# Two-layer cross-attention: the first layer's score products in two key halves of 128 instead of one of 256

## The reference, cut to what matters

```python
h = jnp.concatenate([x, latents], axis=1)
q = (latents @ q_w + q_b).reshape(b, k_len, NH, DH)
kv = (h @ kv_w + kv_b).reshape(b, p + k_len, NH, DH, 2)
kmat, v = (kv[..., 0], kv[..., 1])
attn = jnp.einsum('bkhd,bnhd->bhkn', q, kmat) / DH
full_mask = jnp.concatenate([attention_mask.astype(bool), jnp.ones((b, k_len), bool)], axis=-1)
attn = jnp.where(full_mask[:, None, None, :], attn, -jnp.inf)
attn = jax.nn.softmax(attn.astype(jnp.float32), axis=-1).astype(q.dtype)
attn_out = jnp.einsum('bhkn,bnhd->bkhd', attn, v).reshape(b, k_len, H)
```

## Time and profile before

| what | us |
|---|---|
| median of three runs | 1155.17 |
| profiled execution, its own time | 1155.72 |
| its span, first to last instruction | 1153.5 |
| TensorE busy with products in the span | 1078.4 |
| VectorE, ScalarE, GpSimd busy | 690.8, 648.5, 321.7 |
| first attention | 0 to about 480 |

### The profile page before, as it was taken

One profiled execution on the slowest core, in us unless ns is written; L12 is line 12 of the kernel. 1 busy time (PEld: TensorE's weight loads), 2 busy tenths in 40 slices (PEclk: granted clock), 3 DMA queues, 4 the chain that ended last, 5 costly groups with the idle time before them and its releaser, 6 DMA issues. The chain is left out here.

```text
span 1153.5 us, 27390 instructions
## 1 busy us (share of the span) xinstructions
PE 1078.4 (93%) x8976; PEld 912.7 (79%) x8976; DVE 690.8 (60%) x2683; ACT 648.5 (56%) x2204; POOL 321.7 (28%) x507
## 2 busy tenths in 40 slices
PE   5899999999999998599999999999978999999994
PEld 4788888888888886489899989998966877777772
DVE  4577777777777777562122112211337999999994
ACT  4545555555555555373333333333428999999993
POOL 1223333333333333200000000000001455555555
PEclk9999999999999999789999999999999999999997
DMA  8211111212111110275011010110211212221200
GB/s 287 76 40 49 50 49 57 63 53 65 48 48 48 48 46 10 82 236 158 1 55 54 2 55 19 35 55 1 74 37 59 70 52 67 77 77 50 66 22 28
DMA packets 65355, 71.16 MB, mean 62 GB/s; under 512 B 7056, under 2 KB 41104, under 8 KB 65296
## 3 DMA queue, kind: packets, MB, share of 16 engines
q1 hardware_dynamic: 65296, 70.42, 19.2%
HBM read 49.43 MB, written 20.97 MB: 61 GB/s over the span
## 5 line engine op out<-in xcount | busy, mean ns | idle before, releaser
L727 POOL TENSOR_TENSOR pr<-pr,rec 128x512 f32<-128x512 f32 x128 | 130.6, 1042 | 295.8 <-DVE rec L993 295.8
L1496 ACT ACTIVATE pr<-pr,nmax 128x128 f32<-128x128 f32 x512 | 198.2, 396 | 1.5 <-DVE nmax L1584 1.5
L1926 ACT ACTIVATE g_m<-J,b_part_m 128x256 f32<-128x256 f32 x128 | 60.7, 474 | 216.6 <-PE J L175 216.6
L832 ACT ACTIVATE pr<-pr,nmax 128x256 f32<-128x256 f32 x256 | 126.6, 501 | 3.5 <-DVE nmax L982 3.4
L1584 DVE CUSTOM_DVE_ANT_0 pr<-S,madd 128x128 f32<-128x128 f32 x512 | 114.0, 282 | 2.2 <-issue 1.2
L1903 POOL TENSOR_TENSOR resid_m<-resid_m,b_all_m 128x512 f32<-128x512 f32 x16 | 22.3, 1410 | 326.6 <-DMA resid_m<-in_x 326.6
L1496 ACT ACTIVATION_READ_ACCUMULATOR pr<-pr,nmax 128x1 f32 x512 | 100.2, 196 | 0.0
L982 DVE CUSTOM_DVE_ANT_0 pr<-S,madd 128x256 f32<-128x256 f32 x256 | 92.5, 418 | 8.3 <-PE S L1176 8.1
L175 PE MATMUL J<-nT0hi_m,uphi 128*128 128x256 f32 x256 | 73.0, 285 | 8.5 <-DVE uplo L163 5.1
L175 PE MATMUL J<-hThi,wkhi 128*128 128x256 f32 x256 | 74.8, 292 | 0.8 <-DVE wklo L157 0.8
L175 PE MATMUL J<-nT0hi_m,uplo 128*128 128x256 f32 x256 | 72.6, 284 | 0.0
(11 more groups left out here) (236 smaller groups left out, 3233.6 us busy)
## 6 DMA issues: line engine op xcount, KB each, us to landing
staged<-in_L_xattn_mlp_w SPq DMA_DIRECT2D x16, 512.0 KB, 4.4
rows<-in_ctx SPq DMA_DIRECT2D x16, 256.0 KB, 2.8
rows<-in_x SPq DMA_DIRECT2D x16, 256.0 KB, 3.0
kept_c<-hThi SPq DMA_DIRECT2D x16, 256.0 KB, 2.7
kept_c<-hTlo SPq DMA_DIRECT2D x16, 256.0 KB, 2.8
kept_n<-n_out SPq DMA_DIRECT2D x16, 256.0 KB, 2.4
n_in<-kept_n SPq DMA_DIRECT2D x16, 256.0 KB, 3.8
resid_m<-in_x SPq DMA_DIRECT2D x16, 256.0 KB, 2.9
```

Of the source, the lines that this page charges most:

```text
L727: pool.tensor_tensor(part, part, by.unsqueeze(2).broadcast_to([P, per_bank, keys]), ALU.mult).then_inc(normed, 1)
L832: last = nc.scalar.activation(part, part, ACT.Exp, bias=nmax[slot][:, at], scale=-1.0, accum_out=den[slot][:, at])
L1496: last = nc.scalar.activation(pr[k][:, i, :], pr[k][:, i, :], ACT.Exp, bias=nmax[k][:, i:i + 1], scale=-1.0, accum_out=den[r][:, at:at + 1])
L1926: nc.scalar.activation(g[slot][:, :], J[j][:, 0:PR], ACT.Gelu_apprx_tanh, bias=b1_part[:, f, :]).then_inc(J_taken[j], 1)
```

## The change

In the first layer, `scores` writes each product of 256 keys as two of 128 keys. The two halves are the outer loop: for each c, first all three passes and four strips for keys 0 to 127 (columns 0 to 127 of the head's part of the bank), then the same for keys 128 to 255. The stationary operand is the same in both. The last pass of c = 1 and of the second half raises `S_full[j]`. The products of a round go from 24 to 48, each with its own load of the stationary operand. The branch for L = 1 in this function is not used, since the second attention has its own code.

```diff
@@ -1169,15 +1169,17 @@
                     for c in range(RC):
-                        for qh, kh in PASSES:
-                            for j in range(SB):
-                                strip = slice(32 * j, 32 * (j + 1))
-                                k_ap = KT[s][kh][strip, RC * r + c, :] if L == 0 else KT[s][kh][strip, :, :]
-                                mm = nc.tensor.matmul(S[j][:, c * 256:(c + 1) * 256],
-                                                      QT[s][qh][strip, RC * r + c, :], k_ap,
-                                                      start=(qh, kh) == PASSES[0], stop=(qh, kh) == PASSES[-1])
-                                if c == RC - 1 and (qh, kh) == PASSES[-1]:
-                                    mm.then_inc(S_full[j], 1)
+                        for part in range(2):
+                            for qh, kh in PASSES:
+                                for j in range(SB):
+                                    strip = slice(32 * j, 32 * (j + 1))
+                                    at = slice(part * P, (part + 1) * P)
+                                    k_ap = KT[s][kh][strip, RC * r + c, at] if L == 0 else KT[s][kh][strip, part, :]
+                                    mm = nc.tensor.matmul(S[j][:, c * 256 + part * P:c * 256 + (part + 1) * P],
+                                                          QT[s][qh][strip, RC * r + c, :], k_ap,
+                                                          start=(qh, kh) == PASSES[0], stop=(qh, kh) == PASSES[-1])
+                                    if (c, part) == (RC - 1, 1) and (qh, kh) == PASSES[-1]:
+                                        mm.then_inc(S_full[j], 1)
```

## The result

The changed kernel takes 1172.99 us, the median of four runs (1171.99 to 1176.02), against 1154.63 us for the kernel before in the same comparison (1152.41 to 1156.08). The ratio is 1.0155, with a 95% interval from 1.0132 to 1.0179, so the medians differ by 18.4 us and the interval runs from 15 to 21 us. The forecast was 1172.3 us.

The account below looks back on a forecast made before the run. TensorE was taken to bound the kernel; 32 score rounds at +0.55 us give +17.6 us, less 0.5 hidden, +17.1 on the 1155.17 us median: 1172.3 us, range 1164 to 1184.

Parts of the forecast that it names:

- TensorE bounds the first attention: Steady stretch, 60 to 425 us: TensorE busy 357.99 of 365 us, so a microsecond of its work is one of time.
- A set costs the longer of stream and load: Score rounds: each set costs its stream (0.12 us for 256 columns) or the next set's load (0.11), whichever is longer.
- The 0.11 read from the first two sets of loads: Start of a score round: loads 0.11 us apart with nothing streaming, taken as the price of each 128-key set.
- The lower bound of 0.06: Cost of a 128-key score set from below: 0.06 us, its stream, if loads shrink or hide as the transposes' allow.
- The lead-in: Start of a score round: 0.10 us for the first set's loads until its stream begins.
- the lead-out: End of a score round, last set to next operation: 0.23 us less 0.06 for half a stream, 0.17.
- All 32 rounds count: First attention, prologue and end included: every score round pays +0.55 us, +17.6 us in all.
- Little is hidden: Wait for VectorE's V behind round 0: absorbs some 1.1 us at most over 14 entries; 0.5 us taken.
- The fallback to plain float32: Rival, score sets: narrow fp32r runs at plain float32 rate, 0.22 us a set, +56 us, 1211 us; chance 0.12.
- The hidden loads: Rival, score sets: loads don't bind, a set costs its 0.06 us stream, 1155 to 1156 us; binding less or not 0.07.
- the rule by which load and stream add up: Trainium skill on score sets: loads overlap products only in different row groups; estimated +0.66 us a round or +21 us.
- The 81 ns for a pair of load and product: Skill's middle case for score sets: 0.081 us each, round 1.16 us, +7 us, 1162 to 1163 us.

Follow-up runs that it names:

- the run with quarters: Against the kernel before, each score product of 256 keys written as four of 64 keys in both rounds; 1259.36 us, ratio 1.0908.
- the run with quarters in round 0: Against the kernel before, only round 0's score products split into four of 64 keys, round 1 left as it was; 1197.31 us, ratio 1.0363.

## Why the prediction was right

- **TensorE bounds the first attention, so a longer round is a longer run.** Shown: the span grew by 16.7 us, the period by 1.09 us for each entry, and by 0.53 us with only round 0 split.
- **A set costs the longer of stream and load.** Shown from both sides. With the load halved the pace goes to the stream's 0.060; with 64 moving columns it stays at the load's 0.112; with the load halved under the wide stream nothing changes. The 0.11 read from the first two sets of loads was the right row: it measures 0.112. The lower bound of 0.06, read from the plain float32 loads of transposes, did not carry over to fp32r; why those loads start 0.06 apart was not tested.
- **The lead-in and the lead-out.** The sum came out, 1.48 forecast and 1.49 to 1.50 measured, but in part by luck. The forecast was 0.10 + 11 x 0.11 + 0.17. Measured are 211.60 - 211.44 - 0.11 = 0.05 ahead of the steps, 1.23 in the eleven steps and 212.93 - 212.72 = 0.21 behind the last set. The lead-out hardly shrank with the narrower stream (it was 0.23), so taking off half a stream was wrong; the lead-in was half of what was taken over from the kernel before. The two errors, 0.05 and 0.04, nearly cancel. The round 0 paid 0.58 and not 0.55 because it had been 0.91 and not 0.93; the forecast used the larger for both. That is 16 x 0.02 = 0.3 us of the sum.
- **All 32 rounds count.** Nearly. The very first round starts 1.97 us earlier in the changed kernel's profile (25.15 against 27.12), where weights arrive, and the last one 16.1 later (467.71 against 451.61); with its own 0.58 that is the whole 16.7. The early start is a difference in the prologue before any changed instruction (in the other traces the first round starts anywhere from 25.3 to 27.6 us, and at 30.5 with the key product split), so the rounds and what surrounds them cost 18.7 us from first to last. Of this 17.8 is the rounds, reckoned as 30 at 0.57 and the first two, partly in half clock, at 0.22 and 0.49. The clock is at half for one stretch of 3.4 us more in the prologue, near 37 to 44 us, an estimated 1.6 us, and 0.7 was absorbed: 17.8 + 1.6 - 0.7 = 18.7. The forecast named neither the early start nor the extra stretch at half clock, and that they nearly cancel in the span is luck; at the medians the cost is 18.4 us for 17.1 forecast.
- **Little is hidden.** The forecast took 0.5 us, the periods show 0.05 x 14 = 0.7 us. VectorE did become the waiting side before its V, as told. The wait before the transposes shrank by 0.03 us an entry; where the other 0.02 went wasn't looked for.
- **The rivals.** The fallback to plain float32 is refuted by the pace of 0.112 and by 768 records, not 1536. The hidden loads, and with them the not slower outcome, are refuted by the same pace. So is the rule by which load and stream add up, 0.17 a set: a set takes 0.112, with 128 moving columns and with 64 alike. The 81 ns for a pair of load and product of 128 columns, which the Trainium skill gives (page "TensorE: Matmul & The Clock Gate", section "Back-to-back issue gap"), does not hold for fp32r: the trace has 112.

No version here beats the kernel before: the score products of 256 already hide their loads, and the one run that lies at its time with all the work done, the value product in halves, is no faster.

## What to carry to other kernels

Compare for each product the time that its moving columns stream with the time that the next stationary operand loads; here fp32r took about 0.45 ns a moving column and 0.85 ns a stationary one, so 128 stationary columns want some 250 moving ones (an estimate, 0.112 us over 0.45 ns), in strips as well as at full height. The load of fp32r can be read in an existing trace, as the distance of the first two loads of a round, before anything streams (0.11 us for 128 columns, and so was the pace). Splitting above that width is free (512 into 256), splitting below it costs the whole load for each further product. When many narrow products stand together, the clock and the loop's code size can add to that: some 40 us on top of 60 in the run with quarters.

## What the runs showed that I had not expected

- The granted clock fell to half at the end of 2.8 us of back-to-back 64-column products without a single idle moment, ten times between 91 and 491 us in the run with quarters in round 0, though not behind every such round. Busy time on the page doesn't show this; only the clock column does.
- A loop of 1680 TensorE records in two entries lost 2.6 to 3.6 us at each of five seams, with nine packets in the instruction queue in each turn and 84 in all for 35; one of 1392 records lost nothing and had no packet in the loop's steady part.
- A load's pace is about proportional to its columns, 0.058, 0.085 and 0.112 us for 64 (with 64 moving columns), 96 and 128 columns, although a load's recorded duration is 0.14 to 0.20 us.
